# Routed expert rows summed in device memory by accumulating scatters, in a GNN and mixture-of-experts kernel

## The reference

```python
x = x + _L0_gnn_ref(_layernorm(x), edge_attr_512, path_coeffs, src, dst, path_indices)
x = x + _L0_ffn_ref(_layernorm(x)[None], Wr, sWg, sWu, sWd, Wg, Wu, Wd)[0]

def _L0_ffn_ref(...):            # x: (625, 512)
    for e in range(2):           # shared experts
        shared = shared + silu(x @ sWg[e]) * (x @ sWu[e]) @ sWd[e]
    probs = softmax(x @ Wr); top_w, top_i = top_k(probs, 6); top_w /= sum(top_w)
    gate = zeros((N, 64)).at[arange(N)[:, None], top_i].set(top_w)
    for e in range(64):          # routed experts
        routed = routed + (silu(x @ Wg[e]) * (x @ Wu[e]) @ Wd[e]) * gate[:, e:e + 1]
    return shared + routed + x
```

## Time and profile before

| | us |
|---|---|
| median of 3 runs | 1163.52 (1163.28 to 1169.18) |
| the profiled execution, its own time | 1169.7 |
| its span, first to last instruction | 1168.3 |
| PE busy | 879.1 (75%) |
| DVE busy | 571.5 (49%) |
| POOL busy | 370.3 (32%) |
| ACT busy | 223.0 (19%) |
| HBM read, written | 310.17 MB, 13.63 MB |

### The profile page before, as it was taken

The page is one execution under the profiler, slowest core; times in us unless marked ns, Lnnn a source line. Parts: engine busy times, 40 slices in busy tenths (PEclk is TensorE's granted clock), DMA queues, the critical chain, the costliest instruction groups (busy, mean ns, idle before and its releaser), DMA issues.

```text
span 1168.3 us, 19976 instructions
## 1 busy us (share of the span) xinstructions
PE 879.1 (75%) x7088; PEld 471.9 (40%) x7089; DVE 571.5 (49%) x1289; ACT 223.0 (19%) x567; POOL 370.3 (32%) x419
## 2 busy tenths in 40 slices
PE   0056678677767776796999889989989988998820
PEld 0033334333433443784353454435444543533410
DVE  5199999999999996621111111111111111111128
ACT  1021332133223311200211111111211111112100
POOL 1635225423542500066233223232322322232110
PEclk9999998999899989798899999999999999999975
DMA  7837347634753553504999999999999999999757
GB/s 256 327 115 287 136 155 289 239 149 191 289 206 147 227 217 139 231 2 18 274 378 379 391 389 385 390 394 361 379 391 393 356 382 391 392 387 389 315 130 193
DMA packets 109288, 323.01 MB, mean 276 GB/s; under 512 B 35834, under 2 KB 35987, under 8 KB 86511
## 3 DMA queue, kind: packets, MB, share of 16 engines
q1 hardware_dynamic: 84958, 260.18, 60.3%
q0 software_dynamic: 22368, 57.44, 14.1%
q10 hardware_dynamic: 1826, 3.54, 1.0%
HBM read 310.17 MB, written 13.63 MB: 277 GB/s over the span
## 4 chain that ended last, share of the span: by engine, by line
PE 61%; DVE 11%; issue 10%; DMA 5%; DVEq 4%; POOL 4%; ACT 3%; SPq 0%; ACTq 0%; POOLq 0%
PE ps L1035 21%; PE ps L1078 10%; PE ps L544 10%; DVE big L527 7%; PE ps L985 4%; PE ps L741 3%; POOL pair_d L858 3%; PE ps L578 3%; PE ps L1054 2%; DMA big<-y_d 2%; DVEq L525 2%; PE ps L1029 2%; DVEq L518 2%; PE ps L562 2%; PE ps L1110 2%
## 5 line engine op out<-in xcount | busy, mean ns | idle before, releaser
L527 DVE TENSOR_TENSOR big<-big 128x512 f32 x640 | 393.5, 688 | 31.0 <-DMA big<-xn_d,idx 27.2
L1035 PE MATMUL ps<-big 128*64 128x512 f32 x1024 | 244.6, 621 | 34.5 <-issue 33.5
L544 PE MATMUL ps<-big,mixed 128*32 128x256 f32 x2560 | 169.4, 410 | 105.0 <-DVE big L527 105.0
L294 POOL DMA_INDIRECT big<-xn_d,idx x160 | 154.6, 966 | 232.7 <-DVE big L527 161.2
L1045 DVE TENSOR_TENSOR mixed<-big,ps 128x256 f32<-128x256 f32 x64 | 27.0, 422 | 328.9 <-ACT big L1042 328.9
L950 POOL DMA_INDIRECT big<-h_d,Lg x64 | 62.5, 977 | 297.5 <-issue 297.5
L544 PEld LDWEIGHTS ps<-big,mixed 128*32 128x32 f32 x2560 | 79.9, 117 | 189.9 <-DVE big L527 79.1
L1035 PEld LDWEIGHTS ps<-big 128*64 128x64 f32 x1024 | 70.4, 142 | 167.8 <-issue 167.8
L1078 PE MATMUL ps<-big,mixed 128*64 128x256 f32 x1024 | 124.6, 385 | 0.0
L1002 POOL DMA_INDIRECT y_d<-big,sia x74 | 75.7, 1023 | 109.8 <-DVE big L1091 99.4
L1078 PEld LDWEIGHTS ps<-big,mixed 128*64 128x64 f32 x1024 | 67.9, 136 | 35.3 <-issue 2.6
(11 more groups left out here) (161 smaller groups left out, 652.0 us busy)
## 6 DMA issues: line engine op xcount, KB each, us to landing
big<-in_L_ffn_Wg SPq DMA_DIRECT2D x64, 1024.0 KB, 11.1
big<-in_L_ffn_Wu SPq DMA_DIRECT2D x64, 1024.0 KB, 13.9
big<-in_L_ffn_Wd SPq DMA_DIRECT2D x64, 1024.0 KB, 17.0
big<-in_edge_attr SPq DMA_DIRECT2D x10, 4096.0 KB, 16.6
big<-y_d SPq DMA_DIRECT2D x5, 1344.0 KB
big<-xn_d,idx POOLq DMA_INDIRECT x160
big<-in_L_ffn_sWg SPq DMA_DIRECT2D x2, 1024.0 KB, 5.5
big<-in_L_ffn_sWu SPq DMA_DIRECT2D x2, 1024.0 KB, 7.2
```

The source lines that it names most:

```text
L294: pool.indirect_dma_start(xs[s][:, c, :], None, xn_d[:, :], bass.IndirectOffsetOnAxis(ap=table[:, c0 + c:c0 + c + 1], axis=0)).then_inc(x_ ...
L527: ins = dve.tensor_tensor(pr[k % 2][:, :, EXT * p:EXT * (p + 1)], xs[s][:, :, ds(o1, EXT)], es[s][:, :, ds(o2, EXT)], ALU.mult)
L544: ins = pe.matmul(bank(BA)[WIN * h:WIN * (h + 1), h0:h0 + HP * EXT], onehot[s][:, CW * h + r, :], pr[k % 2][:, CW * h + r, :], start=r == ...
L1035: ins = pe.matmul(bank(k2)[TA * h:TA * (h + 1), :].rearrange("p (w f) -> p w f", w=2), xgT[k2][:, k, 0:TA], gu[:, :, k, W * h:W * (h + 1)] ...
```

## The change

The sum is kept in one tensor in memory, `acc_d` (N rows and 256 spare ones, 512 wide).

- After L726, ACT stores X (x + H) into `acc_d` (two transfers, `st_xh`). `add_0` then overwrites X with shared expert 0 instead of adding, the first time after that store has landed.
- Each item's scatter adds its rows to `acc_d`. Two experts may hold the same row, and such adds must not overlap: before its scatter, POOL waits until that of the item before has landed in full (both of its signals).
- The pair's own number goes; the records hold 2 x row and 4 x row instead. An empty slot is no longer dropped: the minimum with `spare` gives it a spare row of its own, to which it adds zeros. So each scatter moves all 128 pieces.
- In quads 2, 5, 8, 11 and 14, at s = 0, POOL also waits for `down_1` of block b, adds block b of X to `acc_d` in one transfer of 125 rows, and waits until it has landed, all ahead of that item's scatter.
- At the end SP copies `acc_d` to the output in one transfer. The read-back, DVE's sums and the ten stores are gone.

```diff
@@ constants, setup
-    G(pool.iota(pay4[:, :, 1]..., pattern=[[BP * TOPK, NB], [1, TOPK]], base=0, channel_multiplier=TOPK))
-    G(pool.memset(pay4[:, :, 3], 0))
-    G(pool.memset(fill[:, :, :], 0))
+    for c, m in ((1, 2), (3, 4)):
+        G(pool.iota(pay4[:, :, c].rearrange("p (b k) -> p b k", b=NB), pattern=[[m * BP, NB], [0, TOPK]],
+                    base=0, channel_multiplier=m))
+    G(pool.memset(fill[:, :, :], 1 << 20))
...
-    G(pool.memset(fill[:, :, 0:2], 1 << 20))
+    G(pool.memset(fill[:, :, 2], 0))
...
+    for k, m in ((0, 2), (1, 4)):
+        V(dve.tensor_scalar(spare[:, k:k + 1], tcol[:, :], float(N + k * P), float(m), ALU.add, ALU.mult))
@@ routing
     V(dve.tensor_tensor(X[:, :, :], X[:, :, :], H, ALU.add))
     v_xh = V.n
+    after(act, V)
+    s_acc, n_acc = load(act, "st_xh", *rows(lambda r: (acc_d[0:N, :].rearrange("(b p) d -> p b d", p=BP)[r], X[r])))
...
-        V(dve.tensor_tensor(X[:, b, :], X[:, b, :], bank(BD)[0:BP, :], ALU.add))
+        if b == 0:
+            dve.wait_ge(s_acc, n_acc)
+        V(dve.tensor_copy(X[:, b, :], bank(BD)[0:BP, :]))
@@ expert stage
-    def scatter(t, s, at_):
+    def scatter(t, s, at_, before, block=None):
         more = has_more(pool, t)
+        if before:
+            pool.wait_ge(*before)
+        if block is not None:
+            pool.wait_ge(ye_ok, block + 2)
+            pool.dma_start(acc_d[BP * block:BP * (block + 1), :], X[:, block, :], accum_op=ALU.add
+                           ).then_inc(sh_out, 16)
+            pool.wait_ge(sh_out, 16 * block + 16)
         pool.wait_ge(y_ok, t + 2)
...
-            pool.indirect_dma_start(y_d.rearrange("r (h d) -> (r h) d", d=w),
+            pool.indirect_dma_start(acc_d.rearrange("r (h d) -> (r h) d", d=w),
                                     bass.IndirectOffsetOnAxis(ap=row_of(k), axis=0),
                                     yb[s][:, k * D // 2:k * D // 2 + w], None,
-                                    bounds_check=NPAIR * D // w - 1, oob_is_err=False
+                                    bounds_check=(N + 2 * P) * D // w - 1, compute_op=ALU.add
                                     ).then_inc(y_out[s], 16)
...
-            scatter(t, s, a)
+            before = (y_out[s - 1], 32 * i + 64) if s > 0 else None if at(i, 0) else (y_out[3], 32 * i + 32)
+            scatter(t, s, a, before, add if s == 0 else None)
...
-        dve.tensor_scalar(sia[:, k, :], Ls[:, k, :, 1], 2.0 + 2.0 * k, half[:, k:k + 1],
-                          ALU.mult, ALU.add).then_inc(sia_ok, 1)
+        dve.scalar_tensor_tensor(sia[:, k, :], Ls[:, k, :, 1 + 2 * k], spare[:, k:k + 1],
+                                 half[:, k:k + 1].broadcast_to([P, E]), ALU.min, ALU.add).then_inc(sia_ok, 1)
@@ end
-    yl = [load(sync, f"ld_y{b}", *rows(lambda r, b=b: (yall[r, b], yv[r, b]))) for b in range(NB)]
-    for b in range(NB):
-        dve.wait_ge(*yl[b])
-        VV(dve.tensor_reduce(tot[:, b, :], yall[:, b].rearrange("p k d -> p d k"), axis=AX.X, op=ALU.add))
-        VV(dve.tensor_tensor(X[:, b, :], X[:, b, :], tot[:, b, :], ALU.add))
-        after(act, V)
-        outs.append(load(act, f"st_out{b}", *rows(lambda r, b=b: (ov[r, b], X[r, b, :]))))
+    sync.wait_ge(sh_out, 16 * NB)
+    o = load(sync, "st_out", tuple(m.rearrange("r d -> (r d)").rearrange("(a c) -> a c", a=160)
+                                   for m in (out, acc_d[0:N, :])))
```

More of the change, by code:

```diff
@@ L77, in gnn_moe @@
     assert UG * PP == P and UG * NSEG == P and E // 4 > EARLY + 2 * NB
-    NPAIR = N * TOPK
     LPP = -(-(E * CAP + TB) // P)
@@ L218, in gnn_moe @@
     half = sb("half", [P, 2])
+    spare = sb("spare", [P, 2])
     sia = sb("sia", [P, 2, E], I32)
     mrow = sb("mrow", [1, E + 1], I32)
-    yall = ring[0:BP, 0:NB * TOPK * D].rearrange("p (b k d) -> p b k d", b=NB, k=TOPK)
     ps = nc.alloc_psum_tensor("ps", [P, 8 * 512], F32)
@@ L230, in gnn_moe @@
     pair_d = nc.dram_tensor("pair_d", [P * LPP, 4], I32).ap()
-    y_d = nc.dram_tensor("y_d", [NPAIR, D], F32).ap()
+    acc_d = nc.dram_tensor("acc_d", [N + 2 * P, D], F32).ap()
     ct_d = nc.dram_tensor("ct_d", [TCR, 4], I32).ap()
@@ L331, in gnn_moe @@
                 base=0, channel_multiplier=1))
-    G(pool.iota(pay4[:, :, 1].rearrange("p (b k) -> p b k", b=NB), pattern=[[BP * TOPK, NB], [1, TOPK]],
-                base=0, channel_multiplier=TOPK))
-    G(pool.memset(pay4[:, :, 3], 0))
-    G(pool.memset(fill[:, :, :], 0))
+    for c, m in ((1, 2), (3, 4)):
+        G(pool.iota(pay4[:, :, c].rearrange("p (b k) -> p b k", b=NB), pattern=[[m * BP, NB], [0, TOPK]],
+                    base=0, channel_multiplier=m))
+    G(pool.memset(fill[:, :, :], 1 << 20))
     G.own()
@@ L468, in gnn_moe @@
     VV(dve.scalar_tensor_tensor(half[:, 1:2], tcol[:, :], float(3 * TC), half[:, 1:2], ALU.is_ge, ALU.add))
+    for k, m in ((0, 2), (1, 4)):
+        V(dve.tensor_scalar(spare[:, k:k + 1], tcol[:, :], float(N + k * P), float(m), ALU.add, ALU.mult))
+    V.own()
     v_sel = V.n
@@ L906, in gnn_moe @@
     sia_ok = sem("sia_ok")
+    sh_out = sem("sh_out")
     he_ok = sem("he_ok")
@@ L923, in gnn_moe @@
     after(pool, V, max(v_flags, v_xh))
+    pool.wait_ge(s_acc, n_acc)
     sync.wait_ge(s_pair, 16 * NB * TOPK)
@@ L1085, in down @@
             for k in (0, 1):
-                dve.tensor_scalar(si[s][:, k:k + 1], Ls[:, k, ds(at_, 1), 1], 2.0 + 2.0 * k, half[:, k:k + 1],
-                                  ALU.mult, ALU.add)
+                dve.scalar_tensor_tensor(si[s][:, k:k + 1], Ls[:, k, ds(at_, 1), 1 + 2 * k], spare[:, k:k + 1],
+                                         half[:, k:k + 1], ALU.min, ALU.add)
         dve.wait_ge(dn_ok, t + 5)
@@ L1126, in first_items, with quad @@
                 gather(s, 4 + s, 4 + s)
-    def quad(i, left, at_=None, up=None, dn=None):
+    def quad(i, left, at_=None, up=None, dn=None, add=None):
         for s in range(4):
@@ L1158, in gnn_moe @@
         quad(i, min(10, E - 4 * i), up=i // 3 if i % 3 == 0 and i // 3 < NB else None,
-             dn=i // 3 if i % 3 == 1 and i // 3 < NB else None)
+             dn=i // 3 if i % 3 == 1 and i // 3 < NB else None,
+             add=i // 3 if i % 3 == 2 and i // 3 < NB else None)
     for eng in (sync, act, pool, pe, dve):
@@ L1234, in gnn_moe @@
     pool_ready()
-    dve.wait_ge(ye_ok, NB + 1)
-    for s in range(4):
-        dve.wait_ge(g_in[s], 16 * nquad)
-    yv = y_d.rearrange("(b p k) d -> p b k d", b=NB, k=TOPK)
-    ov = out.rearrange("(b p) d -> p b d", p=BP)
-    tot = H
-    yl = [load(sync, f"ld_y{b}", *rows(lambda r, b=b: (yall[r, b], yv[r, b]))) for b in range(NB)]
-    outs = []
-    for b in range(NB):
-        dve.wait_ge(*yl[b])
-        VV(dve.tensor_reduce(tot[:, b, :], yall[:, b].rearrange("p k d -> p d k"), axis=AX.X, op=ALU.add))
-        VV(dve.tensor_tensor(X[:, b, :], X[:, b, :], tot[:, b, :], ALU.add))
-        after(act, V)
-        outs.append(load(act, f"st_out{b}", *rows(lambda r, b=b: (ov[r, b], X[r, b, :]))))
-    for o in outs:
-        act.wait_ge(*o)
+    sync.wait_ge(sh_out, 16 * NB)
+    o = load(sync, "st_out", tuple(m.rearrange("r d -> (r d)").rearrange("(a c) -> a c", a=160)
+                                   for m in (out, acc_d[0:N, :])))
+    sync.wait_ge(*o)
 _INS = ["x", "src", "dst", "edge_attr_512", "L0_gnn_path_coeffs", "L0_gnn_path_indices", "L0_ffn_Wr",
```

## The result

| | before | after |
|---|---|---|
| median of 4 runs each, us | 1165.71 (1163.28 to 1169.18) | 1200.97 (1198.54 to 1203.19) |
| ratio after / before | | 1.030, 95% interval 1.0261 to 1.0338 |
| profiled execution, its own time and span, us | 1169.7, 1168.3 | 1200.84, 1199.6 |
| expert stage, first scatter to the issue of the end's first transfer, us | 551.8 | 618.1 |
| end, from that issue to the last instruction, us | 43.4 | 5.9 |

The changed kernel is 35 us slower, where the forecast had 13. The two profiled executions are 31.3 us apart in span: stage +66.2, end -37.5, and the stage starts 2.6 us later. That start varies: it lies at 573.1 us in the kernel before and at 575.0 and 570.3 in e1 and e13, which have the same program up to there. The remaining 4 us lie in the profiled execution of before, that much slower than the median of its runs.

What follows compares the result with a forecast made beforehand. The prediction took the 16 DMA engines to bound the expert stage, PE 8% behind. With the change POOL's chain decides: stage +49 us, end -36.4, net +13, giving 1176.5 us, with an 8-in-10 range of 1138 to 1232.

Steps and rivals of the forecast that it cites:

- end saved: After the last scatter: the 43.4 us end gives way to one copy of about 7 us, saving 36.4 us.
- `st_xh`, `add_0`, tables: Before and early in the expert stage: the store of X, the copy in `add_0` and `spare` cost tenths of a us.
- more bytes alone: Expert stage, DMA engines: 2.64 MB more written, without reading destinations, cost 7 us.
- bytes and the destination's read on the engines: Expert stage, full DMA engines: 12.96 MB more with destinations read cost 34 us, giving a stage of 586 us.
- chain, before any extra of adding: POOL in the expert stage: scatters and blocks, each waiting for the last landing, need 559 us.
- the adding's extra to a landing: Each link of POOL's chain: an adding scatter lands 0.7 us later than a plain one, giving 601 us.
- The bound from above: Each link of POOL's chain: adding costs at most one whole further trip through full engines, 3.9 us.
- A single late block costs nothing: POOL in the expert stage: four `yb` buffers allow some three items' lag, 26 us; gathers are issued six ahead.
- What would show it: Signs in the changed trace: scatter landing 7.0 us, DMA share 0.95, weight spacing 9.5 us, DVE's wait for a DMA.
- Rival C: POOL's chain: the destination's read stands in line before the write, 2 us more per link; 1200 to 1254 us, chance 0.19.
- the forecast's own range: Whole kernel: the chain decides with 0.45 to 1.3 us extra per landing; 1165 to 1200 us, chance 0.36.
- B: Expert stage: the destination's read costs engines and landing little, stage +7 us; 1143 us taken together, chance 0.28.

Runs made afterwards that it cites:

- e1: Kernel before, with POOL waiting before each plain scatter until the one before has landed; 1166.99 us, ratio 0.9998.
- e13: Kernel before, with each block of the end's read-back in two transfers of 6 KB to a partition instead of one of 12 KB; ratio 0.9996.
- e14: Changed kernel, but scatters and blocks of X overwrite their destination instead of adding, so the output is not the sum; 1139.18 us, ratio 0.9744.
- e4: Changed kernel with two sums in memory for even and odd items, each scatter waiting for the last but one; 1169.02 us, ratio 1.0014.
- e2: Kernel before, with scatters adding onto rows of their own in zeroed `y_d`, without a chain; 1225.23 us, ratio 1.0495.
- e5: Changed kernel with blocks of X out of the chain: ACT stores them to the output, POOL adds `acc_d` at the end; ratio 1.0088.
- e7: Changed kernel with blocks of X out of the chain, stored to the output by ACT, and empty slots dropped again; ratio 1.0066.
- e10: The kernel of e7 once more, on another chip, beside the changed kernel; ratio 1.0052.
- e3: Changed kernel with a semaphore of its own for each item's second landing, waited for only after two pieces; 1206.91 us, ratio 1.0334.

## Why the forecast had the sign and not the size

The mechanism was the forecast's: POOL waits for landings, DVE's L1104 waits for a DMA, the stage outgrows what the end gives back. The numbers by its steps:

| step | forecast, us | measured, us |
|---|---|---|
| end saved | -36.4 (copy 5 to 9) | -37.5 (copy lands in 5.8, end 5.9) |
| `st_xh`, `add_0`, tables | 0 | stage starts 2.6 later; 0.7 in e14, which has them too, so within the spread |
| more bytes alone | 7 | 5.0, with the chain (e14) |
| bytes and the destination's read on the engines | 34 | 26.5 (e4); 18.7 for 7.68 MB (e2) |
| chain, before any extra of adding | 559, below DMA's 586 | never the bound: 556.8 with it (e14) |
| the adding's extra to a landing | 0.7 in each, none for a block | one piece 1.0, two 2.7, block 1.5 in the changed kernel; 2.3 to 2.6 and 3.8 to 4.7 without a single chain (e2, e4) |
| stage | 601 | 618.1 |

**The end, the bytes, and the engines.** Right, with the engines' share a little too dear. From the queues, 13.5% of 480 us is 64.8 us of all 16 engines for 13.33 MB; in e14 it is 43.7 us for 15.32 MB, 2.85 per MB. Some 50 items' gathers (120 KB each, 5.9 MB) at 2.85 leave 48 us for 7.4 MB added: 6.5 per MB, by this estimate 2.3 times a plain byte. The Trainium skill (Collectives: The Full Stack, "The bandwidth ceiling: the fold count and why AG ≠ RS ≠ AR") puts the slowness of a reducing transfer down to its two source reads, not to the add. The 2.3 is near such a doubling, though no run separates the read from the add. The stage pays only 26.5 us and not 34. The two queues together went to 103.5% in e4 (88.7 + 14.8) from 101.5% in e14, so part of the added engine time may fit in where the weights leave gaps; that is a reading, not shown by a run.

**The failed step is the extra of adding in a landing, "I take 0.7 us", the same for one piece and two, and nothing for a block of X.** It rested on rows that say that size hardly counts in a landing. That holds for plain transfers, also in e14 (6.0 for the scatter, 5.9 for 16 bytes), and it says nothing of adding ones. The traces' signals give the real length, from the start of an item's scatter to the last signal of its two transfers (means of items 8 to 55, us):

| | one piece | two pieces | whose landing POOL waits for |
|---|---|---|---|
| before | 7.5 | 7.4 | none |
| e14, plain | 7.2 | 7.6 | the last item's |
| e2, adding | 9.8 | 11.2 | none |
| e4, adding | 9.8 | 12.3 | the last but one's |
| e5, adding, no blocks | 8.6 | 10.8 | the last item's |
| changed kernel | 8.2 | 10.3 | the last item's |

The plain link was forecast well: 7.2 and 7.6 with 0.87 on top are 8.1 and 8.4, against 8.2 and 8.5. Adding lengthens it by 2.3 us for one piece (e2 over before; 2.6 for e4 over e14) and by 3.8 to 4.7 for two, three times the 0.7 and more. In a single chain it is less: 1.0 and 2.7 in the changed kernel, 1.4 and 3.2 in e5. In part this may be because the chain holds the weights up, so that the engines are less full (share 1.00 from 600 to 1080 us, 1.04 in e4); at an extreme, from 1150 to 1190 us, the share is 0.25 and scatters land after 4 to 6 us. But in the middle of e5's stage the share is 1.03. In e2 and e4 an item's transfers can still be under way when the next item's are issued, which a single chain rules out; no run separates the two. That the spacing of one-piece items came out at 9.09 us beside a forecast of 8.9 is therefore in part luck. A block of X adds 9.5 us where 8.4 stood (it lands in 8.5 us, in e14 in 7.0).

In two-piece items, part of the extra is POOL's own: the second piece comes 1.91 us after the first instead of 1.34 (699.26 to 701.17, 679.99 to 681.33), because each instruction takes 1.6 us. What follows until the next scatter is 10.7 us against 6.5 in the rows shown, on average 9.4 against 7.1. How much of the longer landing is the read of the destination, and how much the longer time that POOL's instruction takes, no run separates.

Against the forecast's 601 us, 43 x 0.2 = 8, 8 x 2.15 = 17 and 5 x 1.3 = 6 us come on top, and the last eight items take 14.6 us less than their share of the sum: 618. The forecast had only the last four on free engines; POOL was so far behind that the weights were all issued (1136.00 us) before item 56's scatter (1150.10). The bound from above that the prediction had for one link, 3.9 us, covers all but e4's two-piece landings.

**The slack.** "A single late block costs nothing" is right for plain transfers, where the blocks are hidden (e14), and wrong once the chain binds (23 us in e5). What the chain costs shows in two places:

| us | e14 | e4 | e5 | changed kernel |
|---|---|---|---|---|
| one expert's weights each (60 on SP's timeline) | 8.86 | 9.20 | 9.24 | 9.53 |
| from the last of these to the end's issue | 35.9 | 37.1 | 51.4 | 57.7 |

From e14 to e4 the weights slow down, which is the price on the engines. From e4 to the changed kernel they slow down by as much again (19 us over the 60), and 21 us come from the stage's last part: POOL is three items behind, and when the weights are through there is nothing left for its lag to hide behind. e5, with one chain and no blocks, shows that second place alone: its weights go at e4's pace, and 14 of its 17 us over e4 are the lag at the end (e7 and e10: 9.23 and 9.25, 50.2 and 50.7). So e10's number came out as expected, but not by its theory that two near bounds slow each other all along.

**What would show it.** Landing of the scatter 7.0 expected, 6.9 shown, which is luck, since it is the median of a mixture (e3); DMA share 0.95 expected and measured; weight loads each 9.5 us expected, 9.53 measured (573.91 to 1136.00 on SP's timeline); DVE waits for a DMA, as the forecast asked. Rival C had the place right too, and with its 2 us nearly the price that e2 and e4 show; in the single chain the extra came out smaller, as the prediction had argued against C, though not shown to be for its reason, freer engines. The measured 1201 us lies where the forecast's own range (1165 to 1200) and C's (1200 to 1254) meet. (The range of 8 in 10 is said to go between the middles of B and C, which by their own ranges are 1140 and 1227, not 1138 and 1232; nothing hangs on it.)

## What to carry to other kernels

Moving a sum into the transfers removed 37.5 us of an exposed end and cost 66 in a stage whose DMA engines were full; the order that the adds need was free by itself, and it was the adding that cost, on the engines and in each landing that the next transfer waits for. The landing of a new kind of transfer can't be taken from rows of another kind: here adding took 1.0 to 2.6 us more for one piece and 2.7 to 4.7 for two, where plain rows suggested nearly nothing. Before such a change, ask whether the engines have room for the read of each destination, and let at least two sums take turns, so that no transfer waits for the one just before it: that alone gave back 40 of the stage's 61 us here, less 9 for the second copy. And an engine that waits is not yet a cost (133 us on POOL in e14). Look at how far it falls behind: it counts where the buffers before it run out (DVE's `yb`), and at the end of the stage, where its lag stands by itself.

## What the runs showed of the hardware

- POOL's instruction for an adding scatter takes 1.60 us against 1.04 for the same plain one, and the 16-byte transfer behind it 1.12 against 0.57 (means over 74 and 54 in the changed kernel and e14). The two overlap: the 16-byte transfer starts 1.08 us after the scatter in both kernels, while a second adding scatter starts 1.91 us after the first and a plain one 1.34.
- An adding scatter of 128 pieces and the 16 bytes behind it land 9.8 us after the scatter's start with the engines full and no wait between items (e2), the same plain in 7.5 (before), and adding ones in 8.2 in a single chain (changed kernel).
- An accumulated byte takes some 2.3 times the engine time of a plain one on q0, an estimate from the queues' shares (6.5 against 2.85 us of 16 engines per MB).
- A copy of 1.28 MB from memory to memory lands in 5.8 us on otherwise free engines; the same copy with adding, at the end of e4, in 9.0 us.
- Where two transfers raise one semaphore, the trace does not tell their landings apart: 6.9 us shown for the scatter, 7.7 with a semaphore for each (e3).
- The read-back into 112 and 13 partitions runs at 244 GB/s with 12 KB and with 6 KB to a partition, against 384 GB/s of the whole mix in the stage, with the engines full in both.
